# Attention with found indices: spreading them over the partitions through DRAM, scores a step earlier

## What is computed

```python
def _token(i, q_i, k, v):                       # per image, head (12) and token (256)
    sim = k @ q_i
    sim = jnp.where(jnp.arange(Tn) <= i, sim, -jnp.inf)
    _, top_idx = jax.lax.top_k(sim, M)          # M = 8
    ...
    for comb in COMBS:                          # sets of one and of two of the eight
        idx = jnp.concatenate([jnp.full((nc, 1), i), top_idx[slots]], axis=1)
        K, V = k[idx], v[idx]
        gram = jnp.einsum('cnd,cmd->cnm', K, K)
        score = log(det(gram) + 1e-6) / (s + 1)
        w = softmax(einsum('cnd,d->cn', K, q_i) / 4)
        out_s = einsum('cn,cnd->cd', w, V)
    probs = softmax(scores)
    y = probs @ outs
```

## Time and profile before

| what | value |
|---|---|
| median of 3 runs | 7131.62 us (7116.27 to 7138.18) |
| the profiled execution | 7141.3 us, its span 7139.7 us |
| TensorE clock granted, mean | 0.767 of full speed |
| PE matmul busy | 5247.7 us (74%) |
| DVE busy | 4446.2 us (62%) |
| POOL busy | 3282.9 us (46%) |
| ACT busy | 2741.4 us (38%) |
| touched phase, first to last score | 1593.8 to 4634.4 us |

### The profile page before, as it was taken

The page is one execution under the profiler, slowest core; times in us unless marked ns, Lnnn a source line. Parts: engine busy times, 40 slices in busy tenths (PEclk is TensorE's granted clock), DMA queues, the critical chain, the costliest instruction groups (busy, mean ns, idle before and its releaser), DMA issues. The chain is left out here.

```text
span 7139.7 us, 151565 instructions
## 1 busy us (share of the span) xinstructions
PE 5247.7 (74%) x50932; PEld 4010.8 (56%) x50933; DVE 4446.2 (62%) x9385; ACT 2741.4 (38%) x6866; POOL 3282.9 (46%) x4341
## 2 busy tenths in 40 slices
PE   5776776978888888888888888750991697349990
PEld 2333334756666666666666666640781575349990
DVE  5777774238888888888888888851664333212223
ACT  3333332225555555555555555521220233223330
POOL 1222222116666666666666666616226000354446
PEclk8677767987777777777777777755995898579995
DMA  4000000000000000000000000012222002111113
GB/s 135 7 5 7 5 2 6 0 7 2 2 2 2 2 2 2 2 2 2 2 2 2 3 2 2 2 25 69 72 76 74 14 0 58 38 56 46 44 43 108
DMA packets 103217, 167.30 MB, mean 23 GB/s; under 512 B 17219, under 2 KB 82508, under 8 KB 101557
## 3 DMA queue, kind: packets, MB, share of 16 engines
q1 hardware_dynamic: 68820, 80.83, 3.8%
q0 software_dynamic: 33792, 78.69, 3.5%
HBM read 85.54 MB, written 73.92 MB: 22 GB/s over the span
## 5 line engine op out<-in xcount | busy, mean ns | idle before, releaser
L2302 POOL TENSOR_TENSOR l2a_prod<-l2a_keys 128x64 f32<-128x64 f32 (+1 forms) x2304 | 1167.5, 536 | 857.9 <-ACT l2a_norms L2194 850.8
L2182 ACT CAST l2a_spread<-l2a_b 128x512 bf16<-128x512 f32 x1536 | 834.3, 603 | 463.0 <-PE l2a_b L2634 285.2
L2634 PE MATMUL l2a_b<-l2a_ident_bf,l2a_index 128*128 128x128 bf16 x6144 | 656.2, 265 | 379.4 <-ACT l2a_spread L2182 329.3
L2651 PE MATMUL l2a_g<-l2a_feat,l2a_onehot 128*128 128x33 bf16 x27648 | 882.8, 185 | 53.8 <-DVE l2a_onehot L2516 49.2
L2651 PEld LDWEIGHTS l2a_g<-l2a_feat,l2a_onehot 128*128 128x128 bf16 x27648 | 857.3, 102 | 64.6 <-issue 58.5
L2634 PEld LDWEIGHTS l2a_b<-l2a_ident_bf,l2a_index 128*128 128x128 bf16 x6144 | 480.8, 119 | 432.4 <-ACT l2a_spread L2182 368.8
L1734 POOL TENSOR_TENSOR l_hc<-l_hs,l_bc 128x512 f32<-128x512 f32 x192 | 243.0, 1266 | 801.4 <-DVE l_hs L1808 793.1
L2618 PE MATMUL l2a_s<-l2a_qkT 32*128 32x128 f32 (+1 forms) x1536 | 558.1, 451 | 47.5 <-issue 47.5
L1903 PE MATMUL l_y<-l_hc,l_selT 128*96 128x512 f32 x384 | 310.8, 904 | 295.9 <-POOL l_hc L1734 295.8
L2525 DVE TENSOR_REDUCE l2a_dots<-l2a_prod 128x72 f32<-128x1152 f32 x384 | 515.5, 1342 | 4.3 <-POOL l2a_prod L2308 4.3
L2516 DVE TENSOR_SCALAR l2a_onehot<-l2a_spread,l2a_key_col 128x2048 bf16<-128x2048 bf16 x576 | 493.3, 884 | 7.5
(11 more groups left out here) (400 smaller groups left out, 11428.6 us busy)
## 6 DMA issues: line engine op xcount, KB each, us to landing
rows_in<-main_zeros SPq DMA_DIRECT2D x1, 13824.0 KB, 59.7
l2f_xg<-rows_in SPq DMA_DIRECT2D x72, 192.0 KB, 2.4
rows_out<-l2f_ys POOLq DMA_DIRECT2D x72, 192.0 KB, 2.4
l3f_xg<-rows_in SPq DMA_DIRECT2D x72, 192.0 KB, 2.4
rows_out<-l3f_ys POOLq DMA_DIRECT2D x72, 192.0 KB, 2.4
l3f_w<-in_l3f_w SPq DMA_DIRECT2D x2, 4608.0 KB
l_xT<-in_l_xT SPq DMA_DIRECT2D x16, 384.0 KB, 3.9
main_x_res<-in_x SPq DMA_DIRECT2D x1, 6144.0 KB, 18.0
```

Source lines behind the costliest of these rows:

```text
L2182: nc.scalar.copy(spread[:, s[2] % 2, 4 * c:4 * c + 4, :], b_ps[c % 2][:, :, :]).then_inc(S["spread_ready"], 1)
L2302: nc.gpsimd.tensor_tensor(made[:, j, at:at + wide * wide, :].rearrange("p (b a) f -> p b a f", b=wide), key[:, lo:lo + wide, :].unsqueeze( ...
L2634: ins = nc.tensor.matmul(b_ps[c % 2][:, k, :], flat_index[:, at:at + 1].broadcast_to([P, P]), ident_bf[:, :], start=True, stop=True)
L2651: ins = nc.tensor.matmul(g_ps[j][:, a * FEAT:(a + 1) * FEAT], onehot[:, s[2] % 2, kt, j * SLOTS + a, :], feat3[:, s[1], kt, piece, h, :], ...
```

## The change

The index operation leaves DVE; so do the 16 matmuls of PE and the four casts of ACT per step. In their place, all in turn s: ACT casts the found numbers to bf16 (`cast_index`); PE turns them, 16 rows of 128, with one matmul, plus one that adds the turned `absent` table where the step is of the first tile (`turn_index`); ACT copies the result to SBUF (`copy_turned`); SP writes the 4 KB to a DRAM row and, when they have landed, reads them back onto all 128 partitions, 4 KB each, into `spread`. The one-hot of turn s+2 waits for this DMA. `score` is issued one step ahead, at the head of PE's turn, and in PE's turn s `turn_index(s)` stands between the two halves of `gather(s-3)`; ACT's `cast_index(s)` stands ahead of its first `take_gathered` and `copy_turned(s)` between the two.

```diff
+        index_rows = nc.dram_tensor("index_rows", (2, 2 * SLOTS * P), BF16).ap()
-        b_ps = [m.ps(f"b{k}", [P, 4, P]) for k in range(2)]
+        t_ps = [m.ps(f"t{k}", [2 * SLOTS, P]) for k in range(2)]
@@ SP
+                def body(n, u, i, back, last):
+                    if isinstance(n, int) and n == B:
+                        return
+                    q, k = count_of((n, u, i)), i % 2
+                    first = isinstance(q, int) and q < 2
+                    if not first:
+                        sp.wait_ge(S["spread_in"], q * 16 - 16)
+                        hold(sp, S["sp_held"])
+                    sp.wait_ge(S["turned_ready"], counted(q + 1))
+                    hold(sp, S["sp_held"])
+                    sp.dma_start(index_rows[k:k + 1, :].rearrange("o (k t) -> (o k) t", k=2 * SLOTS),
+                                 indexT[:, k, :]).then_inc(S["rows_out"], 16)
+                    if not first:
+                        sp.wait_ge(S["onehot_ready"], counted(q - 1))
+                        hold(sp, S["sp_held"])
+                    sp.wait_ge(S["rows_out"], q * 16 + 16)
+                    sp.dma_start(spread[:, k, :, :].rearrange("p k t -> p (k t)"),
+                                 index_rows[k, :].partition_broadcast(P)).then_inc(S["spread_in"], 16)
@@ ACT
-                def copy_spread(s, c):
...
-                    nc.scalar.copy(spread[:, s[2] % 2, 4 * c:4 * c + 4, :], b_ps[c % 2][:, :, :]
-                                   ).then_inc(S["spread_ready"], 1)
+                def cast_index(n, u, i):
+
+                    q = count_of((n, u, i))
+                    act.wait_ge(S["found_ready"], q * 2 + 2)
+                    act.wait_ge(S["turned"], counted(q - 1) if not (isinstance(q, int) and q < 2) else 1)
+                    nc.scalar.copy(index[:, i % 2, :, :], found[:, i % 2, :, :]).then_inc(S["index_ready"], 1)
+
+                def copy_turned(n, u, i):
+
+                    q = count_of((n, u, i))
+                    act.wait_ge(S["turned"], counted(q + 1))
+                    if not (isinstance(q, int) and q < 2):
+                        act.wait_ge(S["rows_out"], q * 16 - 16)
+                    nc.scalar.copy(indexT[:, i % 2, :], t_ps[i % 2][:, :]).then_inc(S["turned_ready"], 1)
...
-                    for half in range(2):
-                        if s1:
-                            copy_spread(s1, 2 * half)
-                            copy_spread(s1, 2 * half + 1)
-                        if s3:
-                            take_gathered(s3, half)
+                    if real:
+                        cast_index(n, u, i)
+                    if s3:
+                        take_gathered(s3, 0)
+                    if real:
+                        copy_turned(n, u, i)
+                    if s3:
+                        take_gathered(s3, 1)
@@ DVE
-                        tt(index[:, i % 2, :, :].rearrange("p j a -> p (j a)"),
-                           found[:, i % 2, :, :].rearrange("p j a -> p (j a)"), absent[:, t, :],
-                           ALU.add).then_inc(S["index_ready"], 1)
...
-                        dve.wait_ge(S["spread_ready"], counted(q * 4 + 4))
+                        dve.wait_ge(S["spread_in"], q * 16 + 16)
@@ PE
+                def turn_index(n, u, i):
+
+                    q = count_of((n, u, i))
+                    pe.wait_ge(S["index_ready"], counted(q + 1))
+                    pe.wait_ge(S["turned_ready"], counted(q - 1) if not (isinstance(q, int) and q < 2) else 1)
+                    near = i // PAIRS == 0
+                    ins = nc.tensor.matmul(t_ps[i % 2][:, :], index[:, i % 2, :, :].rearrange("p j a -> p (j a)"),
+                                           ident_bf[:, :], start=True, stop=not near)
+                    if near:
+                        ins = nc.tensor.matmul(t_ps[i % 2][:, :], absent[:, :], ident_bf[:, :], start=False, stop=True)
+                    ins.then_inc(S["turned"], 1)
...
-                        score(n, u, i)
-                    s1, s3 = back(1), back(3)
-                    for half in range(2):
-                        if s1:
-                            spread_out(s1, 2 * half)
-                            spread_out(s1, 2 * half + 1)
-                        if s3:
-                            gather(s3, half)
+                        if i < STEPS - 1:
+                            score(n, u, i + 1)
+                        elif not last:
+                            score(n + 1, 1 - u, 0)
+                    s3 = back(3)
+                    if s3:
+                        gather(s3, 0)
+                    if not (isinstance(n, int) and n == B):
+                        turn_index(n, u, i)
+                    if s3:
+                        gather(s3, 1)
```

More of the change, by code:

```diff
@@ L2340, in _ @@
                 nc.vector.tensor_copy(mask_bf[:, :], y[:, 0, 0:P])
+                nc.vector.tensor_copy(absent[:, :], absent_in[:, :])
                 nc.vector.memset(tT[HC:HC + 1, :, :], 1.0)
@@ L2500, in body @@
                             dve.wait_ge(S["max_chain"], q * 2 + (j + 1))
+                            if j == 0 and not (isinstance(q, int) and q < 2):
+                                dve.wait_ge(S["index_ready"], counted(q - 1))
                             hold(dve, S["dve_held"])
@@ L2612, in score @@
                         pe.wait_ge(S["a_sb"], counted(n * 8 + 5))
-                    pe.wait_ge(S["searched"], counted(q - 1) if not (isinstance(q, int) and q < 2) else 1)
+                    if not (isinstance(q, int) and q < 2):
+                        pe.wait_ge(S["found_ready"], q * 2 - 2)
                     for j in range(2):
@@ L2622, in score @@
                     ins.then_inc(S["scores_ready"], 1)
-                def spread_out(s, c):
-                    q = count_of(s)
-                    if c == 0:
-                        pe.wait_ge(S["index_ready"], counted(q + 1))
-                    if not (isinstance(q, int) and q == 0 and c < 2):
-                        pe.wait_ge(S["spread_ready"], counted(q * 4 + (c - 1)))
-                    flat_index = index[:, s[2] % 2, :, :].rearrange("p j a -> p (j a)")
-                    for k in range(4):
-                        at = 4 * c + k
-                        ins = nc.tensor.matmul(b_ps[c % 2][:, k, :], flat_index[:, at:at + 1].broadcast_to([P, P]),
-                                               ident_bf[:, :], start=True, stop=True)
-                    ins.then_inc(S["b_psum"], 1)
+                def turn_index(n, u, i):
[8 more added lines that the diff above has]
+                    ins.then_inc(S["turned"], 1)
                 def gather(s, j):
@@ L2676, in _ @@
                     front(0, 0, k)
+                score(0, 0, 0)
                 steps(pe, body)
@@ L2737, in host_layouts @@
     slot = np.tile(np.arange(SLOTS), 2)[None, :]
-    lay["l2a_absent"] = np.stack([np.where(slot >= row, 512.0, 0.0), np.zeros((P, 2 * SLOTS))],
-                                 axis=1).astype(np.float32)
+    lay["l2a_absent"] = np.where(slot >= row, 512.0, 0.0).astype(np.float32)
     last_slot = np.array(list(range(SLOTS)) + [1, 3, 5, 7] + [2, 2, 3, 3, 6, 6, 7, 7] +
```

28 lines of the change are left out of this document (12 added, 16 removed).

## The result

The changed kernel takes 6931.06 us, the median of 4 runs (6921.36 to 6937.07); the kernel before, run between them, takes 7126.69 us (7116.27 to 7138.18). The ratio is 0.9724, 95% interval 0.9703 to 0.9745: about 196 us faster, where 260 were forecast. The profiled execution has a span of 6935.4 us.

The account below looks back on a forecast made before the run. DVE was taken to bound the fourth phase: 242.1 + 179.4 - 72 - 113 = 236 us in the steady stretch, times 1.10 = 260, giving 6870 us. Range 6740 to 7010; likeliest case (58 in 100) 6790 to 6960.

Parts of the forecast that it names:

- Part 1: Index operation L2507 leaves DVE: 179.4 us gained in the steady stretch, 72 us of it coming back at the one-hot.
- Part 2: Scores issued a step ahead on PE: DVE's 242.1 us of waiting for them in the steady stretch go.
- Part 3: 16 matmuls and 4 casts a step leave PE and ACT; new cast and copy 0.3 us each, off DVE's path.
- Part 4: Index path from the search through DRAM to the one-hot two steps on: 8.5 us, hidden, cost taken 0.
- Late indices: Rival, 10 in 100: an index path about twice the assumed 8.5 us limits the image; at 20 us, 7500 in all.
- Part 5: New waits on this step's search in PE's and ACT's order: 3.9 us an image, 113 us in the stretch.
- (a): DVE's dots wait for POOL's products after the second gather, at a step without a stage: 1.0 us an image.
- (b): Steps 10 and 11, heavy on PE and light on DVE: DVE waits for products, weighted 2.4 us an image.
- (c): Scores that are late all the same, on slow stretches: 0.5 us an image.
- clock rival: 13 in 100: PE, with less work, drops its clock in steps 9 to 11; waits 9 us an image, 7035 us.
- No new waits: Rival, 12 in 100: PE and POOL keep up; 6747 us, or 6668 if the 72 us don't come back.
- Gain taken back in the step order: Rival, 7 in 100: waits at other steps too, ACT holding the cast; 9 to 12.5 us an image, 7030 to 7150.

Follow-up runs that it names:

- e1: The kernel before with only its scores issued one step ahead: 7010.47 us, ratio 0.9829.
- e2: The changed kernel with the scores put back in their old place, at the head of their own step: 7278.98 us, ratio 1.0204.
- e5: The changed kernel with every broadcast done twice, the second after the first has landed: 7041.95 us, ratio 0.9871.
- e10: The changed kernel with the third bf16 piece left out of the gather: 6861.03 us, ratio 0.9618.
- e11: The changed kernel with four images in the loop instead of two, so the way back comes half as often: 6916.58 us, ratio 0.9695.
- e4: The changed kernel with 16 thrown-away matmuls of 128 columns on PE before every `turn_index`: 6919.85 us, ratio 0.9703.
- e8: The changed kernel with the stages of the next image one turn earlier on the engines' step lists: 6955.58 us, ratio 0.9747.

## Why the prediction was right, and its size 60 us too large

The time lies in the range and in the likeliest case's own, 6790 to 6960. Per image the sum can be laid beside the traces: scores 8.32 (242.1/29.1) and L2507 6.17 gained, new waits 7.05 and longer one-hots 1.6 (18 x 0.088) lost, other DVE operations 0.7 shorter: 6.5, against the 6.6 measured. ("Almost none" of DVE's idle time lay elsewhere, says the prediction; it was 66 of 354 us in small gaps. They are still there, 64 us, so the sum doesn't suffer.)

- **Part 1, L2507.** The 179.4 us went. The 72 us of excess were said to move to the one-hot. At turn 8 they did: of 2.5 us excess an image 1.47 lay there, and there the one-hots grew by 1.94, since they meet the same weighting. The net return is 46 us (522 x 88 ns) and not 72. The main item the other way is turn 1, where the one-hots fell from 2.85 to 1.44, since they no longer meet POOL's split. The prediction moved the excess as one lump; each turn depends on which POOL operation runs at that moment.
- **Part 2, scores ahead.** Right as to the wait: 242.1 us to nothing; e1 and e2 show that it is this part and that the other can't do without it. Alone, only half of it comes through (e1).
- **Part 3, ACT and PE.** Cast 0.205 and copy 0.252 us for 0.3 each; ACT has time to spare, as said.
- **Part 4, index path.** The cost of nothing held, the length didn't hold everywhere. The transfers are shorter than assumed: 1.4 us for the write (2.4), 3.6 for the broadcast by e5 (4.4). In the rows the broadcast of step 10 is issued at 3081.22, 3.6 us after that step's search ended (3077.62), and so lands about 7.2 after it, for 8.5 in the working; its reader starts at 3090.48, 5.7 us later. But at steps 11 and 0, whose turn waits for a late PE, the same reckoning gives 12.4 and 11.7 us, where the working took one length for all steps; their readers are late as well. By it the slack is least at step 1, read at turn 3: 2.9 us in the median. The working's pair, 10 and 11, for which it left 1 us, has 5.1 in the median and 2.2 at the least. In the whole span DVE waited for the spread four times, 7.0 us, all at the start of the phase (1602.9 to 1614.3); in the steady stretch never. "Late indices" fell as a rival.
- **Part 5, new waits: the term that was mis-sized.** 113 us forecast, 204.5 measured. (a) was 1.0 at turn 3 and is 1.04, in part by luck: from the search's end (3016.61) its chain took 6.1 us for 5.2, and DVE asked at 5.0 for 4.1, so two misses cancel; e10 shows that POOL's load alone would give the same wait. (b) was 2.4 and is 2.03 at turn 0; PE's turn of step 11's index came 10.15 us after F(10), where the working had 8.4 at the fast clock. (c) was 0.5 and is 0. What the working lacked is turn 1 (1.89), turn 2 (0.59), turn 11 (0.51) and DVE's way back (0.96), 3.95 us an image. It stopped at the first reader of PE's lateness: it didn't follow on into turn 1, where PE still runs late and has its own loop end in series, 3.18 us (it stood in the trace of before too, 47.5 us in 14 times from 1700 to 4500, while the score wait lay over it) and then the 1.34 before the gather, which before didn't have. e11 shows that loop end as a cause of turn 1, e10 the gather's length as another.
- **The clock rival.** One half came: the clock is 0.63, below the 0.65 that I named. The other didn't: no score wait. e4 brings the clock back and gains next to nothing, with PE's extra matmuls in the price.
- **No new waits** fell plainly. **Gain taken back in the step order** had 9 to 12.5 us an image of waits; with 7.05 the result lies at the upper edge of my own case, 1 to 7, and by its time inside it. The boundary between the two was drawn finer than the working allowed.
- **Signs.** PE's busy share was to fall by a fifth and rose, from 82% to 84%: its instructions fell from 99 to 85 a step, but the slower clock made each longer. One-hot mean 0.976 us for "about 1.0", image 89.7 for 87 to 89. The waits for POOL's products are 4.7 us an image for "2 to 4", 6.1 with those for the gather. Broadcasts and writes landed sooner than the signs said, and no steady wait for the spread came, as said.

## What to carry to other kernels

A producer issued a step ahead takes a wait away only together with whatever wait now stands in its queue; price both edits jointly, and follow the late engine through every later reader until it has caught up, the loop's end among them. When one wait goes, list what it had covered: here the end of the loop and a POOL operation beside DVE's, both to be read in the trace of before. Where a one-hot meets a running POOL operation, it lasts until that operation is over: read which POOL operation each DVE instruction will meet once it starts earlier or later. Cutting the POOL operation into shorter ones gained 37 us here, though little of it on the one-hots themselves.

## What I had not expected of the hardware

- **DVE's way back and the DMA traffic.** In e1, without broadcasts, DVE shows none before its search (the row of its L2497 has no "issue") and 0.2 us before the index search, though nothing else covers that place there. With the broadcasts it is 27.8 us in 14 times, 2.0 each, and with twice as many (e5) 41.3 in 14, 2.95 each. But e8, with the same broadcasts, has only 7.1 us in 11 times, so the traffic isn't all of it. What links them wasn't tried. It is 28 us of the stretch that no row of before could show.
- **Small transfers.** A 4 KB write to DRAM lands in 1.4 us in the median (1.3 to 4.2), where the 192 KB write of before took 2.4; with twice the broadcasts (e5) in 3.0. A 512 KB broadcast out of one 4 KB row lands in 3.6 us (3.2 to 5.3).
- **A DVE operation that meets a POOL operation.** What it takes longer is what the POOL operation had left, less 0.14 to 0.20 us, for one-hots and for L2507 alike (29 times at turn 8 after the change, 27 times before it); DVE's sums of the products meet the same operations at no cost.
- **The clock and idle work.** 16 matmuls of 128 columns in each step's wait lift the granted clock from 0.63 to 0.83 and leave the time 11 us lower, hardly clear of none.
